# Turning h in two pieces of 768 and 640 columns, with an output product that starts on the first piece

## The chip, the cores and the metric

One Trainium2 chip, one core in use. The metric is the device time in microseconds (us) of one execution; the time before is the median of three runs.

## The reference

The input x is (32, 256, 512): 32 batches of 256 rows, 512 numbers each. Each batch goes through a cross attention with the context, and then each row of 512 through a feed-forward network whose operands are quantised to FP4 in blocks of 16. Cut to what matters here:

```
x = x + xattn(layernorm(x), ctx, ctx, Wt, Wp, Wg, Wz, gamma, beta)
# feed-forward, H = 512, I = 1408
gate = fp4_linear(layernorm(x), w_gate)        # (rows, 1408)
y    = fp4_linear(layernorm(x), w_up)          # (rows, 1408)
h    = silu(gate) * y
x    = x + fp4_linear(h, w_down)               # (rows, 512)
# fp4_linear(a, w) = fp4(a) @ fp4(w).T ; fp4: per block of 16 numbers,
# scale = max|.| / 6, each number rounded to {0, .5, 1, 1.5, 2, 3, 4, 6} * scale
```

## The kernel before

The rows are cut into 64 tiles of 128 rows (tile j, two tiles s = 0 and 1 to a batch i). All weights stay in SBUF. The engines run programs written out by hand, each with its own order; a loop over the batches 1 to 29 (`Fori(1, NB - 2)`) and two copies of its body for the last two batches make up nearly all of the time. Engines meet only at semaphores.

**TensorE (PE)**, per tile j: `scores(j + 2)` makes the attention products of a tile two ahead (L457), `hidden(j, s, c)` for c = 0 to 3 makes gate and up in four groups of 352 columns (L478, 24 matmuls a group), and `output(j - 1)` makes the down projection of the tile before (L489, 33 matmuls). Group c of `hidden` waits until VectorE has taken the group that stood in the same PSUM pair (`h_done`). Between the groups stand two tiny products for the attention's statistics: `group_means` (L465, waits for ScalarE's `rowst`) and `group_spread` (L470).

**What happens to h.** VectorE (DVE) multiplies silu and up into h (`gated`, L1126), takes block maxima and scales, and rounds h in place: `h_y` (L958), `h_snap_add` (L967), `h_snap_back` (L971). ScalarE (ACT) makes the grain of the rounding in between (L749). Then, in the next tile's turn of the loop, h is made ready for the product in two halves of 704 columns (`HPIECES`):

- `h_finish` (DVE, L975) writes hq, the quantised values in f32, one half after the other;
- `h_hi` (ACT, L734) rounds each half to f16, as soon as that half of hq is there;
- `h_lo` (DVE, L1113) subtracts the f16 part from hq, which leaves the low f16 part. It waits for `h_hi` of its half (L1112);
- `turn_h` (SyncE, SP, L383) waits for both halves and issues one transposing DMA of both parts, 22 blocks of 128 x 128, into `hT_parts`. `output` waits for it (`h_turned`).

The order on DVE in the loop body is: snap_add, snap_back, sum_pg, h_finish, h_lo, gated c = 0, normalise2 and the x quantisation of the next tile, gated c = 1, x_finish (its last step writes xq at L975), gated c = 2, x_lo, gated c = 3, then maxima, scales and `h_y` of this tile, residual, moments, and `emit` (L1135), which takes the output product. ACT's order is: copy_p, copy_u, `h_hi`, silu c = 0 (L781), u_moments (which end in `rowst`, L714), silu c = 1, the grain of x, `x_hi` (L728, waits for DVE's xq), silu c = 2, silu c = 3, affine, the grain of h. SP issues, per tile: a load, `turn_h`, `turn_x` (L376, 8 blocks), and the store.

After the last batch nothing is left to overlap: `h_snap_add` to `h_lo` of tile 63 on DVE and ACT, its `turn_h`, its 33 matmuls, its `emit` and its store follow one another.

Of the kernel before, what the change touches and what calls it, by code (L numbers as in the profile page):

```python
# [17 lines left out]
P = 128  # L18
F32 = mybir.dt.float32
F16 = mybir.dt.float16  # L20
BF16 = mybir.dt.bfloat16
# [18 lines left out]
def at_least(eng, sem, n):  # L40

    if isinstance(n, int) and n <= 0:
        return
    eng.wait_ge(sem, n)


def wait_apart(eng, always, sem, n):

    eng.wait_ge(always, 1)
    eng.wait_ge(sem, n)


def build(nc, x, ctx_in, Wt, Wp, Wg, Wz, gamma, beta, w_gate, w_up, w_down, out):
    NB, C, D = x.shape
    H = w_gate.shape[0]
# [5 lines left out]
    KH = H // P  # L63
# [10 lines left out]
    with ExitStack() as stack:  # L74
        def sb(name, shape, dt=F32):
            return stack.enter_context(nc.sbuf_tensor(name, shape, dt))
# [4 lines left out]
        def sem(name):  # L81
            return stack.enter_context(nc.semaphore(name))
# [5 lines left out]
        obank = work[:, 2]  # L88
# [20 lines left out]
        w2 = [w2_parts[:, part] for part in range(2)]  # L109
        up_staged = w2_parts[:].rearrange("p a k n -> p (a k n)").bitcast(F32)  # L110
        raw = sb("raw", [P, 3, HALF])
# [44 lines left out]
        hq = sb("hq", [P, H])  # L156
# [4 lines left out]
        h_row = sb("h_row", [P, 2])  # L161
        h_pow = sb("h_pow", [P, 2])
        o_unit = sb("o_unit", [P, 2])
        hT_parts = sb("hT_parts", [P, 2, KH, P], F16)
        hT = [hT_parts[:, part] for part in range(2)]
        o_sb = early[:, 2 * GW:].rearrange("p (a b) -> p a b", a=2)

        hq_parts = raw[:, 1, 0:H].bitcast(F16).rearrange("p (a k) -> p a k", a=2)
        xq_parts = raw[:, 1, H:H + D].bitcast(F16).rearrange("p (a k) -> p a k", a=2)
        HPIECES = ((0, H // 2), (H // 2, H))  # L170

        first_hm = hT_parts[:, 0].rearrange("p k n -> p (k n)").bitcast(BF16)


        consts_made = sem("consts_made")
# [6 lines left out]
        minus_made = sem("minus_made")  # L182
# [89 lines left out]
        h_t_done = sem("h_t_done")  # L272
        h_r_done = sem("h_r_done")
        hq_ready = sem("hq_ready")
        h_turned = sem("h_turned")
        h_hi_done = sem("h_hi_done")
        h_lo_done = sem("h_lo_done")
        o_done = sem("o_done")
# [65 lines left out]
        def _(sp):  # L344
# [33 lines left out]

            def turn_h(j):

                made = 2 * j + 2 if isinstance(j, int) else sp.to_reg(2 * j + 2)
                wait_apart(sp, minus_made, h_lo_done, made)
                sp.dma_start_transpose(hT_parts[:].rearrange("p a k n -> p (a k) n"),  # L383
                                       hq_parts.rearrange("p a k -> p (a k)")).then_inc(h_turned, 16)

            def store(j, s):
                sp.wait_ge(o_ready, j + 1)
# [53 lines left out]
        def _(pe):  # L441
# [41 lines left out]
            def output(j):  # L483

                at_least(pe, o_ready, j)
                pe.wait_ge(h_turned, 16 * j + 16)
                for k in range(KH):
                    for part, wpart in PARTS:
                        mm = pe.matmul(obank[:, :], hT[part][:, k, :], w2[wpart][:, k, :],  # L489
                                       start=(k == 0 and part == 0 and wpart == 0), stop=(k == KH - 1 and part == 1))  # L490
                mm.then_inc(o_done, 1)

# [195 lines left out]
            body(NB - 2)  # L688
            body(NB - 1)
            output(NT - 1)  # L690


        @block.scalar
        def _(act):
# [33 lines left out]
                nc.scalar.copy(xq_parts[:, 0, :], xq[:, :]).then_inc(x_hi_done, 1)  # L728

            def h_hi(j):  # L730
                at_least(act, h_turned, 16 * j)
                for r, (a, b) in enumerate(HPIECES):
                    act.wait_ge(hq_ready, 2 * j + r + 1)
                    nc.scalar.copy(hq_parts[:, 0, a:b], hq[:, a:b]).then_inc(h_hi_done, 1)  # L734

            def ctx_hi(b):
                act.wait_ge(c_loaded, 16 * b + 16)
# [217 lines left out]
        def _(dve):  # L955
# [154 lines left out]
            def h_lo(j):  # L1110
                for r, (a, b) in enumerate(HPIECES):
                    dve.wait_ge(h_hi_done, 2 * j + r + 1)  # L1112
                    nc.vector.tensor_tensor(hq_parts[:, 1, a:b], hq[:, a:b], hq_parts[:, 0, a:b],  # L1113
                                            ALU.subtract).then_inc(h_lo_done, 1)

            def x_lo(t):
# [432 lines left out]
```

## Time and profile before

| | |
|---|---|
| time, median of 3 runs | 1832.3 us (1831.49 to 1832.64) |
| the profiled execution: its own time | 1831.41 us |
| its span, first to last instruction | 1829.6 us |
| PE, DVE, ACT, POOL busy | 1745.3, 1653.1, 722.8, 800.8 us |
| mean TensorE clock granted | 0.994 |

The span is what the trace shows, the time holds in addition 1.8 us around it. A busy PE is not a PE at its peak: the records of matmuls that follow one another overlap. The waits say more than the busy shares: a view of the waits names, for each engine and line, what it waited for.

### The profile page before, as it was taken

Reading aid. Unit: us, or ns where it says so; the run is one execution under the profiler, and the core shown is the slowest. Engines: PE = TensorE matmul, PEld = TensorE weight load, DVE = VectorE, ACT = ScalarE, POOL = GpSimd, SP = SyncE. Lnnn points to the kernel's source line nnn. Section 1 sums busy time; section 2 is a strip of 40 time slices with the busy share of each in tenths; the row PEclk is TensorE's granted clock in tenths of the full one; section 3 lists DMA queues with packets and bytes.
Section 4 is the critical chain, followed back from the end, with each engine's and each line's share of the span. In section 5 each row is a group of like instructions: output and inputs, shape, how many; then the busy total and the mean of one; then the engine's idle time right before and its main releaser. Section 6 shows DMA issues by size and latency. Waiting matters only on the chain.

```text
span 1829.6 us, 30695 instructions
## 1 busy us (share of the span) xinstructions
PE 1745.3 (95%) x10124; PEld 1097.9 (60%) x10124; DVE 1653.1 (90%) x2629; ACT 722.8 (40%) x1246; POOL 800.8 (44%) x1069
## 2 busy tenths in 40 slices
PE   3799999999999999999999999999999999999996
PEld 2576656666666666566666666665666666666653
DVE  8999999999999999999999999999999999999984
ACT  3564344333434333344334333433433343443331
POOL 6884434344443434444443444443434444343300
PEclk9999999999999999999999999999999999999998
DMA  6112233222322332232233223223322332323122
GB/s 221 34 26 63 51 72 72 70 62 67 72 56 66 72 77 62 60 72 62 66 72 72 62 60 75 66 58 72 72 65 63 71 72 50 72 72 74 42 56 43
DMA packets 281879, 123.04 MB, mean 67 GB/s; under 512 B 252928, under 2 KB 254208, under 8 KB 281856
## 3 DMA queue, kind: packets, MB, share of 16 engines
q1 hardware_dynamic: 281856, 122.74, 28.3%
q8 instruction: 13, 0.21, 0.0%
q14 instruction: 10, 0.08, 0.0%
HBM read 43.03 MB, written 16.78 MB: 33 GB/s over the span
## 4 chain that ended last, share of the span: by engine, by line
PE 43%; DVE 34%; issue 14%; ACT 5%; DVEq 1%; POOL 1%; DMA 1%; ACTq 0%; SPq 0%; POOLq 0%
PE pairs L478 20%; PE work L489 13%; PE pairs L457 5%; DVE hq L975 3%; DVE q L997 3%; DVE h L1126 3%; DVE h L967 3%; ACT early L781 3%; DVE h L958 3%; PE ubank L457 3%; DVE h_amax L979 3%; ACT u_dev L711 1%; DVE x L1026 1%; DVE xn L971 1%; DVE ln_st L1030 1%
## 5 line engine op out<-in xcount | busy, mean ns | idle before, releaser
L478 PE MATMUL pairs<-w_gate_hi,xT_parts 128*128 128x352 f16 x2048 | 628.5, 313 | 12.1 <-DVE h L1126 12.0
L478 PE MATMUL pairs<-w_up_hi,xT_parts 128*128 128x352 f16 x2048 | 627.6, 312 | 0.0
L489 PE MATMUL work<-w_parts,hT_parts 128*128 128x512 f16 x2112 | 468.8, 380 | 12.9 <-DMA hT_parts<-raw 12.9
L489 PEld LDWEIGHTS work<-w_parts,hT_parts 128*128 128x128 f16 x2112 | 207.7, 100 | 250.0 <-issue 17.0
L478 PE MATMUL pairs<-w_up_lo,xT_parts 128*128 128x352 f16 x1024 | 320.0, 312 | 0.0
L478 PE MATMUL pairs<-w_gate_lo,xT_parts 128*128 128x352 f16 x1024 | 319.9, 312 | 0.0
L478 PEld LDWEIGHTS pairs<-w_gate_hi,xT_parts 128*128 128x128 f16 x2048 | 204.9, 100 | 137.7 <-DVE h L1126 23.7
L478 PEld LDWEIGHTS pairs<-w_up_hi,xT_parts 128*128 128x128 f16 x2048 | 200.4, 98 | 97.3
L1126 DVE SCALAR_TENSOR_TENSOR h<-pairs,w_unit,early 128x352 f32<-128x352 f32 x256 | 147.9, 578 | 87.3 <-ACT early L781 87.3
L781 ACT ACTIVATE early<-pairs,w_unit 128x352 f32<-128x352 f32 x256 | 141.1, 551 | 93.0 <-PE pairs L478 93.0
L734 ACT CAST raw<-hq 128x704 f16<-128x704 f32 x128 | 99.4, 778 | 176.1 <-DVE hq L975 174.8
L1392 POOL TENSOR_TENSOR xc<-x_in,c_in 128x512 f32<-128x512 f32 x64 | 163.6, 2576 | 0.0
L1397 POOL TENSOR_TENSOR c_lo<-c_in,c_hi 128x512 fp32r<-128x512 f32 x64 | 94.3, 1494 | 150.8 <-ACT c_hi L739 150.8
L1411 POOL TENSOR_TENSOR att<-rowst,grp 128x1 f32<-128x1 f32 x64 | 38.3, 598 | 268.2 <-DVE grp L1012 268.1
L749 ACT ACTIVATE wm<-h 128x1408 bf16<-128x1408 f32 x63 | 86.8, 1378 | 152.7 <-DVE h L958 152.7
L1433 POOL TENSOR_TENSOR ln_rs<-ln_mv,eps_col 128x1 f32<-128x1 f32 x64 | 13.6, 213 | 298.9 <-DVE ln_mv L1034 298.9
L971 DVE SCALAR_TENSOR_TENSOR h<-wm,h 128x1408 f32<-128x1408 bf16 x63 | 130.1, 2065 | 2.1
L720 ACT ACTIVATE v_sb<-u_sb,att 128x512 f32<-128x512 f32 x64 | 52.1, 814 | 201.5 <-POOL att L1429 201.5
L478 PEld LDWEIGHTS pairs<-w_up_lo,xT_parts 128*128 128x128 f16 x1024 | 100.1, 98 | 52.6
L478 PEld LDWEIGHTS pairs<-w_gate_lo,xT_parts 128*128 128x128 f16 x1024 | 100.1, 98 | 52.5
L975 DVE SCALAR_TENSOR_TENSOR hq<-h,h_unit 128x704 f32<-128x704 f32 x128 | 121.4, 988 | 0.1
L1113 DVE TENSOR_TENSOR raw<-hq,raw 128x704 f16<-128x704 f32 x128 | 108.4, 889 | 3.2
(154 smaller groups left out, 3044.2 us busy)
## 6 DMA issues: line engine op xcount, KB each, us to landing
x_in<-in_x SPq DMA_DIRECT2D x32, 512.0 KB, 3.4
c_in<-in_ctx SPq DMA_DIRECT2D x32, 512.0 KB, 3.5
out<-early SPq DMA_DIRECT2D x64, 256.0 KB, 2.1
raw<-in_L_ffn_w_down SPq DMA_DIRECT2D x2, 1408.0 KB, 8.8
raw<-in_L_ffn_w_gate SPq DMA_DIRECT2D x2, 1280.0 KB, 8.3
w_parts<-in_L_ffn_w_up SPq DMA_DIRECT2D x2, 1280.0 KB, 9.0
xT_parts<-raw SPq DMA_TRANSPOSE x64, 3.1
hT_parts<-raw SPq DMA_TRANSPOSE x64, 5.2
```

The lines of the kernel that those rows point to most:

```text
L457: mm = pe.matmul(dst, wT[wpart][:, k, s * P:(s + 1) * P], src[part][:, k, :], start=(k == 0 and wpart == 0 and part == 0), stop=(k == HT - ...
L478: mm = pe.matmul(pairs[:, pair, n, 0:GW], xT[s][part][:, k, :], w1[n][wpart][:, k, c * GW:(c + 1) * GW], start=(k == 0 and part == 0 and w ...
L489: mm = pe.matmul(obank[:, :], hT[part][:, k, :], w2[wpart][:, k, :], start=(k == 0 and part == 0 and wpart == 0), stop=(k == KH - 1 and pa ...
L734: nc.scalar.copy(hq_parts[:, 0, a:b], hq[:, a:b]).then_inc(h_hi_done, 1)
L749: nc.scalar.activation(m, y, ACT.Abs, scale=GRAIN).then_inc(done, 1)
L781: nc.scalar.activation(silu[:, c % 2, :], pairs[:, pair_of(j, s, c), 0, 0:GW], ACT.Silu, scale=w_unit[:, 0:1]).then_inc(silu_done, 1)
L971: nc.vector.scalar_tensor_tensor(out=y, in0=m, scalar=GRAIN, in1=y, op0=ALU.max, op1=ALU.subtract).then_inc(done, 1)
L975: nc.vector.scalar_tensor_tensor(out=blocks(q_out), in0=blocks(y), scalar=-factor, in1=over_block(scale), op0=ALU.mult, op1=ALU.mult).then ...
L1113: nc.vector.tensor_tensor(hq_parts[:, 1, a:b], hq[:, a:b], hq_parts[:, 0, a:b], ALU.subtract).then_inc(h_lo_done, 1)
L1126: nc.vector.scalar_tensor_tensor(out=h[:, c * GW:(c + 1) * GW], in0=pairs[:, pair_of(j, s, c), 1, 0:GW], scalar=w_unit[:, 1:2], in1=silu[: ...
L1392: nc.gpsimd.tensor_tensor(xc[:, s, :], x_in[:, s, :], c_in[:, s, :], ALU.add).then_inc(xc_ready, 1)
L1397: nc.gpsimd.tensor_tensor(c_parts[1][:, s, :], c_in[:, s, :], c_parts[0][:, s, :].bitcast(F32), ALU.subtract).then_inc(c_ready, 1)
```

## The change

`HPIECES` becomes (0, 768) and (768, 1408), that is 6 and 5 blocks of 128 columns instead of 704 and 704. The hi and lo parts of a piece lie side by side, so that a piece is one contiguous stretch (12 blocks with both parts, then 10). `turn_h` issues one transposing DMA for each piece as soon as `h_lo` of the piece is done, each with its own semaphore. `output` waits for the first before its first matmul and for the second before its 19th. `h_hi` waits before each piece until the earlier transpose of that piece is over. The number of DVE, ACT and PE instructions that compute stays the same; only their sizes change.

```diff
--- before.py
+++ after.py
@@ -161,15 +161,23 @@
         h_row = sb("h_row", [P, 2])
         h_pow = sb("h_pow", [P, 2])
         o_unit = sb("o_unit", [P, 2])
-        hT_parts = sb("hT_parts", [P, 2, KH, P], F16)
-        hT = [hT_parts[:, part] for part in range(2)]
+        hT_parts = sb("hT_parts", [P, 2 * KH, P], F16)
         o_sb = early[:, 2 * GW:].rearrange("p (a b) -> p a b", a=2)
 
-        hq_parts = raw[:, 1, 0:H].bitcast(F16).rearrange("p (a k) -> p a k", a=2)
+        hq_parts = raw[:, 1, 0:H].bitcast(F16)
         xq_parts = raw[:, 1, H:H + D].bitcast(F16).rearrange("p (a k) -> p a k", a=2)
-        HPIECES = ((0, H // 2), (H // 2, H))
-
-        first_hm = hT_parts[:, 0].rearrange("p k n -> p (k n)").bitcast(BF16)
+        HPIECES = ((0, 6 * P), (6 * P, H))
+
+        def hq_part(r, part):
+            a, b = HPIECES[r]
+            return hq_parts[:, 2 * a + part * (b - a):2 * a + (part + 1) * (b - a)]
+
+        def hT(part, k):
+            a, b = HPIECES[0] if k < 6 else HPIECES[1]
+            return hT_parts[:, (2 * a + part * (b - a)) // P + k - a // P, :]
+
+
+        first_hm = hT_parts[:, 0:KH].rearrange("p k n -> p (k n)").bitcast(BF16)
 
 
         consts_made = sem("consts_made")
@@ -272,7 +280,7 @@
         h_t_done = sem("h_t_done")
         h_r_done = sem("h_r_done")
         hq_ready = sem("hq_ready")
-        h_turned = sem("h_turned")
+        h_turned = [sem(f"h_turned{r}") for r in range(2)]
         h_hi_done = sem("h_hi_done")
         h_lo_done = sem("h_lo_done")
         o_done = sem("o_done")
@@ -378,10 +386,10 @@
 
             def turn_h(j):
 
-                made = 2 * j + 2 if isinstance(j, int) else sp.to_reg(2 * j + 2)
-                wait_apart(sp, minus_made, h_lo_done, made)
-                sp.dma_start_transpose(hT_parts[:].rearrange("p a k n -> p (a k) n"),
-                                       hq_parts.rearrange("p a k -> p (a k)")).then_inc(h_turned, 16)
+                for r, (a, b) in enumerate(HPIECES):
+                    made = 2 * j + r + 1 if isinstance(j, int) else sp.to_reg(2 * j + r + 1)
+                    wait_apart(sp, minus_made, h_lo_done, made)
+                    sp.dma_start_transpose(hT_parts[:, 2 * a // P:2 * b // P, :], hq_parts[:, 2 * a:2 * b]).then_inc(h_turned[r], 16)
 
             def store(j, s):
                 sp.wait_ge(o_ready, j + 1)
@@ -483,10 +491,11 @@
             def output(j):
 
                 at_least(pe, o_ready, j)
-                pe.wait_ge(h_turned, 16 * j + 16)
                 for k in range(KH):
+                    if k in (0, 6):
+                        pe.wait_ge(h_turned[k // 6], 16 * j + 16)
                     for part, wpart in PARTS:
-                        mm = pe.matmul(obank[:, :], hT[part][:, k, :], w2[wpart][:, k, :],
+                        mm = pe.matmul(obank[:, :], hT(part, k), w2[wpart][:, k, :],
                                        start=(k == 0 and part == 0 and wpart == 0), stop=(k == KH - 1 and part == 1))
                 mm.then_inc(o_done, 1)
 
@@ -728,10 +737,10 @@
                 nc.scalar.copy(xq_parts[:, 0, :], xq[:, :]).then_inc(x_hi_done, 1)
 
             def h_hi(j):
-                at_least(act, h_turned, 16 * j)
                 for r, (a, b) in enumerate(HPIECES):
+                    at_least(act, h_turned[r], 16 * j)
                     act.wait_ge(hq_ready, 2 * j + r + 1)
-                    nc.scalar.copy(hq_parts[:, 0, a:b], hq[:, a:b]).then_inc(h_hi_done, 1)
+                    nc.scalar.copy(hq_part(r, 0), hq[:, a:b]).then_inc(h_hi_done, 1)
 
             def ctx_hi(b):
                 act.wait_ge(c_loaded, 16 * b + 16)
@@ -1110,7 +1119,7 @@
             def h_lo(j):
                 for r, (a, b) in enumerate(HPIECES):
                     dve.wait_ge(h_hi_done, 2 * j + r + 1)
-                    nc.vector.tensor_tensor(hq_parts[:, 1, a:b], hq[:, a:b], hq_parts[:, 0, a:b],
+                    nc.vector.tensor_tensor(hq_part(r, 1), hq[:, a:b], hq_part(r, 0),
                                             ALU.subtract).then_inc(h_lo_done, 1)
 
             def x_lo(t):
```

SP's program in the first half of the loop body, before. A transpose of 22 blocks stands between the load of x and the transpose of x:

```order
L349 ISA [waits xc_ready,q_norm]
L349 DMA x_in<-in_x 128x2x512
L381 ISA
L383 DMA_TRANSPOSE hT_parts<-raw 128x22x128 [waits h_lo_done,minus_made]
L374 REGISTER_ALU
L376 DMA_TRANSPOSE xT_parts<-raw 128x8x128 [waits x_lo_done,minus_made]
L388 ISA [waits o_ready]
L388 DMA out<-early 128x512
```

The same place now:

```order
L357 ISA [waits xc_ready,q_norm]
L357 DMA x_in<-in_x 128x2x512
L390 ISA
L392 DMA_TRANSPOSE hT_parts<-raw 128x12x128 [waits h_lo_done,minus_made]
L390 REGISTER_ALU
L392 DMA_TRANSPOSE hT_parts<-raw 128x10x128 [waits h_lo_done,minus_made]
L382 REGISTER_ALU
L384 DMA_TRANSPOSE xT_parts<-raw 128x8x128 [waits x_lo_done,minus_made]
L396 ISA [waits o_ready]
L396 DMA out<-early 128x512
```

One row of 22 blocks has become two, of 12 and of 10, each behind its own value of `h_lo_done`. Nothing else on SP has changed places.

ACT's program, the two casts of `h_hi` between the copy of u (L703, now L712) and silu c = 0 (L781, now L790), before:

```order
L703 ACTIVATE u_sb,u_sum<-ubank 128x512 [waits v_ready,u_done]
L734 CAST raw<-hq 128x704 [waits hq_ready,h_turned]
L734 CAST raw<-hq 128x704 [waits hq_ready]
L781 ACTIVATE early<-pairs,w_unit 128x352 [waits h_done,gu_done]
L709 ACTIVATE rowst<-u_sum 128x1 [waits u_copied,sq_steps,grp_done]
```

And now:

```order
L712 ACTIVATE u_sb,u_sum<-ubank 128x512 [waits v_ready,u_done]
L743 CAST raw<-hq 128x768 [waits hq_ready,h_turned0]
L743 CAST raw<-hq 128x640 [waits hq_ready,h_turned1]
L790 ACTIVATE early<-pairs,w_unit 128x352 [waits h_done,gu_done]
L718 ACTIVATE rowst<-u_sum 128x1 [waits u_copied,sq_steps,grp_done]
```

The first cast has grown from 704 to 768 columns, the second has shrunk to 640 and has one more semaphore to wait for. On DVE the four instructions L975, L975, L1113, L1113 stand where they stood and change their sizes in the same way.

PE's program at the output product in the loop, before:

```order
L470 MATMUL ubank<-att,gmean 128x1 [waits grp_copied,sq_steps]
L489 MATMUL work<-w_parts,hT_parts 128x512 [waits h_turned,o_ready]
L489 MATMUL work<-w_parts,hT_parts 128x512 x32
L686 REGISTER_ALU
L686 COMPARE_AND_BRANCH
L457 MATMUL pairs<-q_hi,wpT_hi 128x512 [waits q_ready,h_done]
```

And now:

```order
L478 MATMUL ubank<-att,gmean 128x1 [waits grp_copied,sq_steps]
L498 MATMUL work<-w_parts,hT_parts 128x512 [waits h_turned0,o_ready]
L498 MATMUL work<-w_parts,hT_parts 128x512 x17
L498 MATMUL work<-w_parts,hT_parts 128x512 [waits h_turned1]
L498 MATMUL work<-w_parts,hT_parts 128x512 x14
L695 REGISTER_ALU
L695 COMPARE_AND_BRANCH
L465 MATMUL pairs<-q_hi,wpT_hi 128x512 [waits q_ready,h_done]
```

The 33 matmuls are the same, in the same order; a second wait stands before the 19th.

## Rows read from the trace of the kernel before

**Rows 1.** The page: span and busy time of each engine

```profile
span 1829.6 us, 30695 instructions
...
PE 1745.3 (95%) x10124; PEld 1097.9 (60%) x10124; DVE 1653.1 (90%) x2629; ACT 722.8 (40%) x1246; POOL 800.8 (44%) x1069
```

**Rows 2.** 300 us of the loop: PE, PEld, DVE, ACT, POOL busy (calls)

```profile
200.00:500.00 300.00, 295.93 (x1719) 184.06 (x1718) 276.67 (x451) 119.38 (x208) 129.59 (x178) 1.00 0.29 67
```

**Rows 3.** Waits of PE and DVE, 200 to 1780 us

```profile
PE ubank L465 <- ACT rowst L714: 12.4, 29, 0.4
PE pairs L478 <- DVE h L1126: 9.9, 29, 1.4
...
DVE h L1126 <- ACT early L781: 76.7, 64, 2.3
```

**Rows 4.** DVE in order of time, 880 to 960 us

```profile
889.60 1.69 DVE L975 SCALAR_TENSOR_TENSOR hq<-h,h_unit 128x704 f32<-128x704 f32 x2
891.33 1.69 DVE L1113 TENSOR_TENSOR raw<-hq,raw 128x704 f16<-128x704 f32 x2
892.94 0.57 DVE L1126 SCALAR_TENSOR_TENSOR h<-pairs,w_unit,early 128x352 f32<-128x352 f32 x1
...
926.18 0.69 DVE L975 SCALAR_TENSOR_TENSOR xq<-xn,x_scale 128x512 f32<-128x512 f32 x1
928.09 0.58 DVE L1126 SCALAR_TENSOR_TENSOR h<-pairs,w_unit,early 128x352 f32<-128x352 f32 x1 [1.22 <-ACT early L781]
...
945.96 0.58 DVE L1126 SCALAR_TENSOR_TENSOR h<-pairs,w_unit,early 128x352 f32<-128x352 f32 x1
```

**Rows 5.** ACT in order of time, same stretch

```profile
890.51 1.58 ACT L734 CAST raw<-hq 128x704 f16<-128x704 f32 x2 [1.93 <-DVE hq L975]
...
926.98 0.62 ACT L728 CAST raw<-xq 128x512 f16<-128x512 f32 x1 [2.29 <-DVE xq L975]
927.50 0.55 ACT L781 ACTIVATE early<-pairs,w_unit 128x352 f32<-128x352 f32 x1
```

**Rows 6.** Durations by line: ns min/median/max

```profile
L975 DVE SCALAR_TENSOR_TENSOR hq<-h,h_unit x128: 877/884/1355, 137.2 to 1808.2; 128x704 f32<-128x704 f32 x128
L975 DVE SCALAR_TENSOR_TENSOR xq<-xn,x_scale x64: 691/691/1643, 85.1 to 1771.1; 128x512 f32<-128x512 f32 x64
...
L734 ACT CAST raw<-hq x128: 777/778/782, 152.8 to 1809.2; 128x704 f16<-128x704 f32 x128
...
L728 ACT CAST raw<-xq x64: 617/618/622, 88.2 to 1771.8; 128x512 f16<-128x512 f32 x64
```

**Rows 7.** The two transposing DMAs: issue in ns, us to landing

```profile
L383 SPq DMA_TRANSPOSE hT_parts<-raw x64: 3237/3342/3398, 155.4 to 1811.0; - x64
...
DMA to landing us min/median/max: 5.1/5.2/6.9
...
L376 SPq DMA_TRANSPOSE xT_parts<-raw x64: 1232/1232/1391, 89.8 to 1774.1; - x64
...
DMA to landing us min/median/max: 3.0/3.1/3.2
```

**Rows 8.** Chain that ended last, from 1780 us: start, us, what

```profile
1786.72 0.78 DVE raw L1113
...
1809.23 1.70 DVE raw L1113 x2
...
1810.99 5.17 DMA hT_parts<-raw
...
1816.30 10.01 PE work L489 x33
```

**Rows 9.** Weight loads of the last tile's output

```profile
1816.27 0.14 PEld L489 LDWEIGHTS work<-w_parts,hT_parts 128*128 128x128 f16 x2 [13.34 <-issue]
...
1821.80 4.00 PEld L489 LDWEIGHTS work<-w_parts,hT_parts 128*128 128x128 f16 x19 [0.28 <-issue]
```

**Rows 10.** 4 us near the end, columns as in Rows 2, then clock

```profile
1807.00:1811.00 4.00, 0.00 (x0) 0.00 (x0) 3.79 (x5) 1.52 (x2) 0.00 (x0) 0.65 0.00 0
```

## The prediction

> **What bounds the kernel now.** The page comes first [rows 1]: PE is busy for 95% of the span, DVE for 90%. In a stretch from the middle of the loop PE is busy for 295.93 of 300 us and DVE for 276.67 [rows 2]. This looks like a kernel bound by PE, and it is nearly one. The view of the waits says otherwise [rows 3]. Between 200 and 1780 us PE waits 29 times for `rowst` before `group_means` (12.4 us, 0.43 each) and 29 times for DVE's `gated` before a group of `hidden` (9.9 us): once each in a batch of two tiles, in 29 batches. DVE, in the same stretch, waits 64 times for ACT's silu (76.7 us, 1.2 each) and never for PE.
>
> What is this wait of DVE for silu? The timelines of DVE and ACT show one instance [rows 4, 5]. DVE writes xq at 926.18; ACT, whose order puts `x_hi` ahead of silu c = 2, has waited 2.29 us for xq, casts it at 926.98 and runs silu at 927.50; DVE goes on with `gated` at 928.09. So the wait starts from DVE's own work and comes back to DVE over ACT, and PE has no part in it. DVE's program with its trips to ACT is a closed ring that sets the period: `gated` c = 0 starts at 892.94 in one batch and at 945.96 in the next, 53.02 us [rows 4]. PE keeps up with some 0.4 us to spare in a tile. What makes DVE's ring longer is paid in every tile; what comes earlier on SP, the DMA queues or PE inside the loop is worth nothing.
>
> A second regime is the end. There the chain is: `h_lo` at 1809.23 for 1.70 us, the transpose from 1810.99 for 5.17, and 33 matmuls from 1816.30 for 10.01 [rows 8]. Each step waits for all of the one before.
>
> **The change in the loop: earlier transposes.** The first DMA can be issued one `h_lo` piece earlier. In the loop nothing waits for it: of PE's waits between 200 and 1780 us none is for `hT_parts` [rows 3]. Worth 0, hidden by PE's own groups c = 0 to 3. The second DMA costs SP one more issue; SP issues 22 blocks in 3.342 us and 8 in 1.232 [rows 7], 0.151 a block with almost nothing fixed, so two pieces take what one took. `turn_x` stands behind it on SP, and needs `x_lo`, for which DVE has three `gated` and the whole quantisation of x to do first. Cost 0. PE's new wait before matmul 19 has long been met and costs 0; ACT's new wait too.
>
> **The change in the loop: the sizes on the ring.** This is the part that I think decides. `h_finish` writes hq in two pieces, ACT casts the first as soon as it stands, and DVE's `h_lo` begins with this first piece. So between the start of `h_finish` and the start of `h_lo` there are two paths: DVE's two pieces of hq (the sum of both, unchanged), and the first piece of hq followed by the first cast. With halves the two are even. From [rows 4, 5]: hq starts at 889.60 and both pieces end at 891.29. The first piece takes 0.884 us [rows 6], to 890.48; ACT starts at 890.51, takes 0.778, and ends at 891.29 as well; `h_lo` starts at 891.33. A first piece of 768 columns makes the second path longer and leaves the first as it is.
>
> How much longer: DVE's same instruction takes 884 ns for 704 columns and 691 for 512 [rows 6], 1.005 ns a column, 64 ns for 64 columns. ACT's cast takes 778 ns for 704 and 618 for 512 [rows 6], 0.833 a column, 53 ns. Together 0.118 us: `h_lo` would start at 891.45. What follows doesn't win it back: the two pieces of `h_lo` together have as many columns as before; the second cast is through by 892.2, before the second `h_lo` could start (892.3); and `gated` c = 0 waits for `h_lo` alone.
>
> How often: `h_lo` runs in the loop body for 62 tiles. The waits of PE for DVE and ACT, two in a batch, mark 29 batches, 58 tiles, as bound by this ring [rows 3]. I add the last two tiles, where the chain that ended last runs over `h_lo` [rows 8], and leave the first two, where DVE hasn't yet become the later one. 60 x 0.118 = **7.1 us lost**. Bounds: 0 if something absorbs it; above, in tiles in which GpSimd slows the first piece of hq (1355 ns for 704 columns at most [rows 6], 1.92 a column), the 64 columns would cost 0.123 on DVE and not 0.064. In one tile of each batch that is 30 x 0.06 = 1.8 more. I take 7.1, since the extra columns are at the piece's end, when GpSimd is mostly done.
>
> **The change at the end.** The first `h_lo` starts 0.12 later, at 1809.35, and takes 0.95 for 768 columns (0.890 plus 64 more at the rate above), to 1810.30; the transpose is issued 0.06 later as now, at 1810.36, 0.63 earlier than 1810.99 [rows 8]. Landing takes 5.2 us for 22 blocks and 3.1 for 8 [rows 7]: 0.15 a block on 1.9, so 3.7 for 12 blocks, 1.5 less. PE starts at 1814.2 instead of 1816.3. The second piece is issued when SP is through with the first (1812.2) and lands 3.4 later, at 1815.6; PE wants it at about 1820.8. So the end is **2.1 us shorter**. Bounds: a landing of 3.1 (as 8 blocks) gives 2.7, one of 5.2 gives 0.6.
>
> The matmuls there start on a slow clock. PE's clock goes from full to the lower of its two levels (1.2 and 2.4 GHz) before the transpose lands: the mean granted is 0.65 in 1807 to 1811 [rows 10], which puts the fall near 1808.2. In the product 13 weight loads from 1816.27 to 1821.80 are 0.425 us apart, and the rest 0.216 [rows 9]. With the pause before the product's first weight load shortened from 13.3 us [rows 9] to 11.2 the fall, at 1808.2, still comes first, so I keep the 13 slow matmuls. The Trainium skill, TensorE: Matmul & The Clock Gate, "Part 1: The HAM clock gate", says that this number changes from run to run, and names 6, 11 and 14 slow matmuls for one kernel; this trace has one such product, with 13, and can't show the spread. By that page's 6 the sum would be 1.5 us lower, by its 14 0.2 higher.
>
> **Sum.** 7.1 - 2.1 = 5.0 us. Against the profiled execution's own time, 1831.41 (span 1829.6 and 1.8 around it), that is 1836.4; the median of the runs is 0.9 above that execution, so the forecast for the median is 1832.3 + 5.0 = **1837.3 us**, 0.27% slower. A measurement of this kernel can tell about 0.2%, 3.7 us, from no change.
>
> **The rivals.**
> - *Slack on DVE absorbs the delay* (not slower). This needs a wait of DVE behind `h_lo` that doesn't hang on `h_lo`, of at least 0.12 us in a tile. For it: the busy shares, PE 98.6% and DVE 92% [rows 2]. Against it: all of DVE's waits of any size are the trip over ACT, which starts from DVE. Then only the end counts: 1832.3 - 2.1 = 1830.2, with bounds 1829.6 and 1831.7. Chance 0.10, a third of it below the 0.2%.
> - *Half of the tiles absorb it*: the tile of a batch in which GpSimd works beside DVE gives the time back, because GpSimd goes on while DVE waits, and slows DVE less after. 30 x 0.118 - 2.1 = +1.4, 1833.7. Chance 0.10.
> - *The clock comes back earlier at the end*: 6 slow matmuls in place of 13 save 7 x 0.21 = 1.5. The sum is +3.5, 1835.8, on the edge. The only recovery in the rows took 5.5 us. Chance 0.08.
> - *The change does not do at the end what it says*: the two transposes share the DMA engines, and the first lands when a single one would have (5.2 after issue). Gain 0.6; +6.5, 1838.8. Speaking for it: only that no row shows two transposes in flight. Chance 0.07.
> - *A second wait on the ring*: the second cast, now with two semaphores and started after a longer first one, ends after 892.3 and holds the second `h_lo`, or GpSimd slows the longer piece. 0.03 to 0.1 us a tile, 2 to 6 us more: about 1841. Margin now 0.15 us a tile. Chance 0.09.
> - *The forecast* as summed: 0.56, with a range of its own of 1835.7 to 1839.
>
> **How the numbers follow.** The forecast is slower by over 0.2% in nearly nine of ten of its cases, since its terms may be off by 1.3 us (0.50 of 0.56); the slow clock's case in half (0.04), the two dearer cases fully (0.16): slower 0.70. Faster: 0.04. Same: the rest, 0.26. A range from 1833.3 to 1840.5 leaves out the first rival, half of the dearest and little else.
>
> **What the profile of the changed kernel would show.** Right: the period from `gated` c = 0 to the same of the next batch at 53.26 instead of 53.02; DVE's `h_lo` of the first piece starting 0.16 after hq's end, not 0.04, with ACT's cast as releaser, some 10 us of idle time in all; PE's waits for `rowst` and `gated` longer by as much; hq pieces of 948 and 820 ns, casts of 831 and 725; at the end the first transpose landing 3.7 after its issue and PE starting 5 us after the first `h_lo` does. Wrong: a period of 53.02 (absorbed); a later start of the second `h_lo` than the first's end (dearer); a landing of over 4.5 us at the end.

## The result and the profile after

The changed kernel takes 1837.72 us in the median of 7 runs (1837.55 to 1838.74), the one before 1831.49 in 7 runs (1830.93 to 1832.99). The ratio is 1.0033 with a 95% interval from 1.0022 to 1.0045: slower by 6.2 us, forecast 5.0. The profiled execution has a span of 1836.4 us and a time of 1838.19; before they were 1829.6 and 1831.41, so that the two traces, 6.8 us apart, hold the whole difference.

The page of the changed kernel, its head (answers to [rows 1]), and its waits of PE and DVE between 200 and 1780 us (to [rows 3]; engine, line, what it waited for, total us, times, longest):

```profile
span 1836.4 us, 30886 instructions
...
PE 1744.1 (95%) x10124; PEld 1097.4 (60%) x10124; DVE 1655.7 (90%) x2629; ACT 717.0 (39%) x1246; POOL 788.1 (43%) x1069
```

```profile
DVE h L1135 <- ACT early L790: 75.0, 62, 2.3
...
PE pairs L486 <- DVE h L1135: 20.9, 29, 1.5
...
PE ubank L473 <- ACT rowst L723: 11.1, 29, 0.4
...
DVE raw L1122 <- ACT raw L743: 10.0, 60, 0.2
```

The busy times have hardly moved. What has moved are waits. A row is there that wasn't: DVE's `h_lo` (now L1122) waits for ACT's cast 60 times, 0.17 us each. And PE waits for DVE's `gated` 20.9 us in place of 9.9, and for `rowst` 11.1 in place of 12.4: 9.7 us more for the two together.

DVE of the changed kernel in order of time, the same place in a batch as in [rows 4], with the two starts of `gated` c = 0 that bound a batch, and ACT's casts (to [rows 5]):

```profile
893.54 1.69 DVE L984 SCALAR_TENSOR_TENSOR hq<-h,h_unit 128x768 f32<-128x768 f32 x2
895.39 1.69 DVE L1122 TENSOR_TENSOR raw<-hq,raw 128x768 f16<-128x768 f32 x2 [0.16 <-ACT raw L743]
897.00 0.58 DVE L1135 SCALAR_TENSOR_TENSOR h<-pairs,w_unit,early 128x352 f32<-128x352 f32 x1
...
950.38 0.58 DVE L1135 SCALAR_TENSOR_TENSOR h<-pairs,w_unit,early 128x352 f32<-128x352 f32 x1
```

```profile
894.52 1.46 ACT L743 CAST raw<-hq 128x768 f16<-128x768 f32 x2 [2.18 <-DVE hq L984]
```

From the start of hq to the start of `h_lo` it is 895.39 - 893.54 = 1.85 us; it was 891.33 - 889.60 = 1.73 [rows 4]. That is the 0.12 of the forecast. But the batch, from 897.00 to 950.38, takes 53.38 us, and the forecast had 53.26.

The end, as the chain that ended last (start, us, what; to [rows 8]), and the weight loads of the last output (to [rows 9]):

```profile
1816.84 0.97 DVE hq L984
...
1817.88 0.84 ACT raw L743
...
1818.75 0.97 DVE raw L1122
...
1819.78 3.72 DMA hT_parts<-raw
...
1823.64 9.43 PE work L498 x33
```

```profile
1823.61 0.14 PEld L498 LDWEIGHTS work<-w_parts,hT_parts 128*128 128x128 f16 x2 [11.28 <-issue]
...
1827.86 4.70 PEld L498 LDWEIGHTS work<-w_parts,hT_parts 128*128 128x128 f16 x22 [0.28 <-issue]
```

The transpose of 12 blocks lands 3.72 us after its issue where 22 took 5.17. From the start of the last hq to the first matmul it is 1823.64 - 1816.84 = 6.80 us; it was 8.86 (1816.30 less 1807.44, the start of the last hq before). The product itself takes 9.43 us where it took 10.01: 10 weight loads 0.425 apart, where there were 13.

**Where the 6.8 us are.** In the two traces, from the first `h_lo` of the loop (tile 1) to that of tile 62 it was 1610.6 us before (176.13 to 1786.72), and is 1620.1 now (176.01 to 1796.12): 9.5 lost in 61 tiles. The way from there to the last hq is 20.72 us in both. The end gives 2.06 back by the earlier start and 0.58 by three fewer slow matmuls. 9.5 - 2.6, and 0.1 less before the loop, is 6.8.

### The profile page after: what moved, and what is told of

Read it like the earlier page. It is cut to its first block, busy times and chain, and to the rows that moved or that the text cites. A ratio compares the mean times of both kernels' runs of the same rounds, so it can differ in the third digit from the quotient of the medians.

```text
span 1836.4 us, 30886 instructions
## 1 busy us (share of the span) xinstructions
PE 1744.1 (95%) x10124; PEld 1097.4 (60%) x10124; DVE 1655.7 (90%) x2629; ACT 717.0 (39%) x1246; POOL 788.1 (43%) x1069
## 4 chain that ended last, share of the span: by engine, by line
DVE 60%; issue 22%; PE 8%; ACT 6%; DVEq 2%; DMA 1%; POOL 0%; ACTq 0%; SPq 0%; POOLq 0%
DVE h L976 5%; DVE h L967 5%; DVE h_amax L988 5%; DVE h L1135 4%; PE pairs L486 4%; DVE hq L984 4%; ACT raw L743 3%; DVE xn L980 2%; DVE ln_st L1039 2%; DVE x L1035 2%; DVE x_amax L988 2%; DVE x_scale L991 2%; DVE xq L984 2%; DVE raw L1127 2%; DVE xn L976 2%
## 5 line engine op out<-in xcount | busy, mean ns | idle before, releaser
L498 PE MATMUL work<-w_parts,hT_parts 128*128 128x512 f16 x2112 | 468.2, 380 | 10.8 <-DMA hT_parts<-raw 10.8
L790 ACT ACTIVATE early<-pairs,w_unit 128x352 f32<-128x352 f32 x256 | 141.1, 552 | 84.9 <-PE pairs L486 84.9
L743 ACT CAST raw<-hq 128x768 f16<-128x768 f32 (+1 forms) x128 | 93.4, 777 | 183.9 <-DVE hq L984 183.9
L1406 POOL TENSOR_TENSOR c_lo<-c_in,c_hi 128x512 fp32r<-128x512 f32 x64 | 81.7, 1297 | 149.3 <-ACT c_hi L748 149.3
L984 DVE SCALAR_TENSOR_TENSOR hq<-h,h_unit 128x768 f32<-128x768 f32 (+1 forms) x128 | 121.4, 988 | 0.1
L1122 DVE TENSOR_TENSOR raw<-hq,raw 128x768 f16<-128x768 f32 (+1 forms) x128 | 108.4, 888 | 10.8 <-ACT raw L743 10.8
```

What stands on the lines that cost most here:

```text
L498: mm = pe.matmul(obank[:, :], hT(part, k), w2[wpart][:, k, :], start=(k == 0 and part == 0 and wpart == 0), stop=(k == KH - 1 and part == 1))
L743: nc.scalar.copy(hq_part(r, 0), hq[:, a:b]).then_inc(h_hi_done, 1)
L790: nc.scalar.activation(silu[:, c % 2, :], pairs[:, pair_of(j, s, c), 0, 0:GW], ACT.Silu, scale=w_unit[:, 0:1]).then_inc(silu_done, 1)
L984: nc.vector.scalar_tensor_tensor(out=blocks(q_out), in0=blocks(y), scalar=-factor, in1=over_block(scale), op0=ALU.mult, op1=ALU.mult).then ...
L1122: nc.vector.tensor_tensor(hq_part(r, 1), hq[:, a:b], hq_part(r, 0), ALU.subtract).then_inc(h_lo_done, 1)
```

## The experiments

Each run of the kernel before on the same chips had medians of 1830.6 to 1831.4 us; ratios are to those. Twelve runs follow, of eleven kernels: one was run twice.

### Sizes without a second DMA: sizes_alone

```diff
-        HPIECES = ((0, H // 2), (H // 2, H))
+        HPIECES = ((0, 6 * P), (6 * P, H))       # in the kernel before, nothing else
```

> The kernel before with pieces of 768 and 640 columns for hq, the cast and h_lo, and still one transposing DMA after both and one wait in the output. My theory (the first piece and its cast lie on a ring of DVE and ACT that sets the period): h_lo starts 0.16 us after the end of hq in every tile, the period is 53.38 us as in the changed kernel, the loop loses its 9.5 us, and the end gains nothing (0.1 lost): about 1841 us, 3 more than the changed kernel. The rival (the second DMA and the added waits cost the time in the loop, the sizes nothing): 1831.5, as before.

Measured: 1842.24 us against 1830.94, ratio 1.0063 (1.0049 to 1.0076). The steps from one `h_lo` to the next are the changed kernel's to 0.01 us, 25.13 and 28.23 in turn, where before they were 25.01 and 28.01. The whole loss in the loop is there without a second DMA and without a second wait on PE, ACT or SP. The time is 1.2 above the 1841 expected.

### Two DMAs without the sizes: hi_then_lo

```diff
-                made = ...(2 * j + 2)
-                wait_apart(sp, minus_made, h_lo_done, made)
-                sp.dma_start_transpose(hT_parts[...], hq_parts[...]).then_inc(h_turned, 16)
+                for part, done in enumerate((h_hi_done, h_lo_done)):
+                    made = ...(2 * j + 2)
+                    wait_apart(sp, minus_made, done, made)
+                    sp.dma_start_transpose(hT_parts[:, part], hq_parts[:, part, :]).then_inc(h_turned[part], 16)
...
+                pe.wait_ge(h_turned[0], 16 * j + 16)     # 22 matmuls with the high part
...
+                pe.wait_ge(h_turned[1], 16 * j + 16)     # then 11 with the low part
```

> Two transposing DMAs and two waits in the output, but halves of 704 columns as before: the first DMA takes all 11 blocks of the high part as soon as ACT has cast both halves, the second the low part; the output does its 22 matmuls with the high part first. My theory: the loop is as before (period 53.02); at the end the first DMA is issued 1.0 us earlier and lands in 3.55 and not 5.17, so that PE starts 2.6 us earlier, and the slow clock's matmuls stay 11 to 13: 1828.9 us. The rival (DMAs and waits cost the loop 9.5 us): about 1838.5.

Measured: 1828.18 us against 1830.94, ratio 0.9985 (0.9976 to 0.9994). The loop has the steps of before, 25.01 and 28.0. The end, as the chain of this kernel, starts its product 6.29 us after the last hq (before 8.86):

```profile
1807.03 0.90 DVE hq L979
...
1808.03 1.51 ACT raw L738 x2
...
1809.61 3.58 DMA hT_parts<-raw
...
1813.32 6.24 PE work L489 x22
1819.56 2.39 PE work L493 x11
```

ACT's cast of both halves releases the DMA, `h_lo` is no longer on the way. Seven matmuls run at the lower clock here, where I had expected 11 to 13. This is the first version that beats both kernels: it keeps what the change gains and has nothing of what it costs.

### The ring opened: silu_first and silu_first_pieces

```diff
-                        if c == 1 and (more or s == 0):
+                        if c == 2 and (more or s == 0):
                             x_hi(j + 1)                  # behind silu c = 2 on ACT, in the loop body
```

> The kernel before with one move on ACT: silu c = 2 runs before x_hi and not behind it. DVE's wait of 1.22 us a tile, which I take for part of a ring without PE, should shrink to about 0.1. My theory (DVE's ring sets the period, PE has 0.8 us to spare in a batch of 53.02): the loop becomes bound by PE at about 52.2 us a batch, some 24 us less in all, 1808 us (1804 to 1814). The rival (PE is the bound of the loop in truth and DVE's waits are idle time without a price): 1831.5.

> The same move on ACT made in the changed kernel (768 and 640 columns, two DMAs). My theory: with DVE's ring no longer the bound, the 0.12 us that the sizes add to a tile is absorbed and only the gain at the end is left, so that this is 2.6 us faster than silu_first: about 1805 us. The rivals (the change costs PE or the DMA queues time in the loop whatever bounds it): 6 us slower than silu_first.

Measured: silu_first 1799.17 us, ratio 0.9824 (0.9811 to 0.9837); silu_first_pieces 1799.58, 0.9829 (0.9817 to 0.9842). The waits of silu_first between 200 and 1740 us:

```profile
DVE h L1126 <- ACT early L781: 22.8, 61, 2.4
...
DVE raw L1118 <- ACT raw L728: 15.3, 58, 0.3
...
PE pairs L478 <- DVE h L1126: 1.3, 1, 1.3
```

And those of silu_first_pieces, of the same stretch:

```profile
DVE h L1135 <- ACT early L790: 19.3, 61, 2.4
...
DVE raw L1127 <- ACT raw L737: 15.4, 58, 0.3
...
DVE raw L1122 <- ACT raw L743: 9.9, 60, 0.2
...
PE pairs L486 <- DVE h L1135: 1.5, 1, 1.5
```

PE waits once in the whole stretch where it waited twice a batch. The period is 51.93 us in both kernels, 24.51 and 27.42 in turn. So DVE's ring set the period, and a trip of 1.2 us over ACT was worth 32 us of the whole; I had expected 24, since I had put PE's own need at 52.2 a batch and not at 51.9, and 1799.17 lies below the range of 1804 to 1814 that I had given.

The second kernel is the sharper test. It has the same 0.16 us before `h_lo` in each of 60 tiles as the changed kernel, 9.9 us in all, and its period is not longer by 0.01. The same pieces cost the loop 9.5 us where DVE is the bound and nothing where PE is.

One part of the expectation failed: silu_first_pieces should have been 2.6 us faster than its partner, and was 0.4 slower, well within the noise of the two intervals. Its last output does start 2.0 us earlier (1782.95 against 1784.92), but takes 10.01 us and not 8.70: 13 slow matmuls against 7. The next two groups follow this up.

### Does PE's slow clock hide the gain at the end? silu_warm and silu_warm_pieces

```diff
             body(NB - 1)
+            pe.wait_ge(h_done, GROUPS * NT)
+            pe.wait_ge(o_ready, NT - 1)
+            for n in range(42):
+                pe.matmul(pairs[:, 0, 0, :], minus_ident[:, :], w2[0][:, n % KH, :], start=True, stop=True)
             output(NT - 1)
```

> silu_first (halves of 704, one DMA) with 42 matmuls of 512 columns on PE that nothing reads, between the output of tile 62 and that of tile 63, so that PE does not rest in the wait at the end. Silu_first had 7 slow matmuls in the last output (8.7 us for 33), the changed kernel 10, before and silu_first_pieces 13. My theory: with no slow matmul the output takes 7.1 us; 1.6 us less than silu_first's profile, 1797.6 us. It serves as the base of the next run.

> The same 42 matmuls in silu_first_pieces (the change). Silu_first_pieces started its last output 2.0 us earlier than silu_first, but took 10.0 us for it and not 8.7, and was no faster in the median. My theory: only the number of slow matmuls hid the gain; with none in either this is 2.0 us faster than silu_warm: 1795.6 us. If something else eats the gain at the end: equal to silu_warm.

Measured: silu_warm 1801.24 us (1797.2 to 1801.33), silu_warm_pieces 1796.42 (1795.11 to 1797.6). The first missed: it is slower than silu_first. Its weight loads at the end:

```profile
1773.01 8.76 PEld L693 LDWEIGHTS pairs<-w_parts,minus_ident 128*128 128x128 f16 x42 [1.40 <-issue]
1784.95 0.34 PEld L489 LDWEIGHTS work<-w_parts,hT_parts 128*128 128x128 f16 x3 [3.18 <-issue]
1785.49 0.15 PEld L489 LDWEIGHTS work<-w_parts,hT_parts 128*128 128x128 f16 x1 [0.20 <-issue]
...
1788.82 4.63 PEld L489 LDWEIGHTS work<-w_parts,hT_parts 128*128 128x128 f16 x22 [0.19 <-issue]
```

PE rests 3.18 us between the last filling matmul and the output; the first three loads are close, then come loads 0.425 apart. The clock fell about when the output began: the mean granted is 0.91 in 1782 to 1786 and 0.66 in 1786 to 1790. In silu_warm_pieces, with the same 42 matmuls, the rest is 1.10 us, and no load is slow. The pair therefore differs by more than the start, and by itself says nothing of the 2.0 us.

### The same with equal rests: silu_warm52, silu_warm_pieces_again, silu_warm_hilo

The filling has 52 matmuls in silu_warm52 and 38 in silu_warm_hilo, which joins silu_first and hi_then_lo.

> silu_warm with 52 filling matmuls and not 42. Silu_warm missed its purpose: PE rested 3.2 us between the last filling matmul and the last output, the clock fell at its start, and 9 matmuls were slow (8.98 us for the output, 1801.2 us in the median), while with the change's earlier transpose (silu_warm_pieces, a rest of 1.1 us) none was slow (7.30, 1796.4). With 52 the rest is about 1 us. My theory: no slow matmul, 7.2 us for the output, and a time 2.0 us above silu_warm_pieces, that is 1798.4 on the same chip. If the gain at the end were no gain: equal to silu_warm_pieces.

> The same kernel as silu_warm_pieces, on the same chip as silu_warm52, as its partner: 1796.4 us.

> The version to which the experiments point: silu c = 2 ahead of x_hi, halves of 704 columns, the high part turned first and the low part second (hi_then_lo), 38 filling matmuls. In hi_then_lo the last output started 6.2 us after the last hq, in the pieces 6.8, in the halves with one DMA 8.9. My theory: 0.6 us faster than silu_warm_pieces at the end, and 0.1 in each of the last two tiles: 1795.6 us; the rival, that the two are equal since the loop is bound by PE in both: 1796.4.

Measured: silu_warm52 1797.23 us (1797.11 to 1799.6), silu_warm_pieces_again 1795.48 (1795.27 to 1796.43), silu_warm_hilo 1795.09 (1794.74 to 1797.48). Weight loads at the end of silu_warm52, then of silu_warm_pieces_again:

```profile
1772.76 10.92 PEld L693 LDWEIGHTS pairs<-w_parts,minus_ident 128*128 128x128 f16 x52 [1.40 <-issue]
1784.70 6.82 PEld L489 LDWEIGHTS work<-w_parts,hT_parts 128*128 128x128 f16 x33 [1.02 <-issue]
```

```profile
1772.98 8.76 PEld L702 LDWEIGHTS pairs<-w_parts,minus_ident 128*128 128x128 f16 x42 [1.40 <-issue]
1782.86 6.82 PEld L498 LDWEIGHTS work<-w_parts,hT_parts 128*128 128x128 f16 x33 [1.12 <-issue]
```

The products take 7.30 us in both, and with the clock out of the way the earlier transpose is worth 1.75 us of 2.0 expected; in the traces the product starts 7.07 us after `h_lo` in the one and 4.88 in the other, 2.2 less. Silu_warm_hilo is the fastest kernel of the study, ratio 0.9805 (0.9792 to 0.9819) to the kernel before; its lead of 0.4 on silu_warm_pieces_again is not clear of the noise.

### The wait before h_lo filled: norm_between

```diff
                     h_finish(j - 1)
+                    if quant_x:
+                        normalise2(j + 1)
                     h_lo(j - 1)
                     for c in range(GROUPS):
                         gated(j, s, c)
                         if c == 0 and quant_x:
-                            normalise2(j + 1)
                             x_first(j + 1)              # in the changed kernel
```

> The changed kernel with one move on DVE: normalise2 of the next tile (0.53 us, ready long before) stands between h_finish and h_lo instead of behind gated c = 0, so that DVE has work while ACT casts the first piece. My theory: the idle 0.16 us before h_lo goes, also the 0.08 by which instructions that wait for nothing overlap; a tile is 0.24 shorter than in the changed kernel and 0.12 shorter than before, and the gain at the end stays: 1837.7 - 60 x 0.24 = 1823 us, 8 faster than before; what GpSimd does to DVE may move it by 2. If the cost of the change in the loop were not this wait: 1837.7.

Measured: 1821.89 us, ratio 0.995 (0.9937 to 0.9964). DVE of this kernel around `h_finish`:

```profile
887.39 1.69 DVE L984 SCALAR_TENSOR_TENSOR hq<-h,h_unit 128x768 f32<-128x768 f32 x2
889.00 0.54 DVE L1049 TENSOR_SCALAR xn<-x,ln_mv,ln_rs 128x512 f32 x1
889.45 1.69 DVE L1122 TENSOR_TENSOR raw<-hq,raw 128x768 f16<-128x768 f32 x2
891.05 0.58 DVE L1135 SCALAR_TENSOR_TENSOR h<-pairs,w_unit,early 128x352 f32<-128x352 f32 x1
```

No idle time stands before `h_lo`; each instruction starts some 0.09 us before the one ahead has ended, as do those that wait for nothing. The steps are 24.74 and 27.95, 52.69 a batch where the changed kernel has 53.36. The change's whole loss in the loop is gone, and more, with all of the change in place.

Not all of this gain is the wait. From the start of hq to the start of the block maxima of x (`x_amax`, L988) it is 4.16 us here (887.39 to 891.55) and 4.53 in the changed kernel (893.54 to 898.07), 0.37 less where I had expected 0.24. The further 0.12 comes from normalise2 itself: in the changed kernel the maxima, which read its result, start 0.57 us after it, and here the next instruction starts 0.45 after it. The kernel before should gain this 0.12 too; it was not run with the move. Behind this stretch, in the tile in which GpSimd works on the context, 0.10 is lost again (from `x_amax` to `gated` c = 1 it is 4.61 us, in the changed kernel 4.51). The 0.25 that is left is still more than the 0.12 that the change had added to a tile, so DVE stood idle for a cast that it could have worked beside.

### Why 9.5 and not 7.1: sizes_736

```diff
-        HPIECES = ((0, H // 2), (H // 2, H))
+        HPIECES = ((0, 736), (736, H))           # in the kernel before
```

> The kernel before with pieces of 736 and 672 columns (32 more and less, where the change has 64) and one transposing DMA. sizes_alone showed the step from one h_lo to the next 0.12 longer in one tile of a batch and 0.23 in the other. If all of it is the path over the first piece and its cast, both are proportional to the columns: 0.06 and 0.115 longer, 5 us in all. If the part above 0.12 is a step, because a different DVE instruction falls under GpSimd's, 0.06 and either 0.06 or 0.17: 3.6 or 6.9 us in all.

Measured: 1832.59 us against 1830.64, ratio 1.0013 (1.0004 to 1.0023). The steps are 25.07 and 28.01: 0.06 longer in one tile, as expected, and not longer at all in the other. Neither of my two accounts had this. The stretch in question lies behind `gated` c = 0 in the tile in which ACT casts the context (L739) and GpSimd then subtracts it (L1397, `ctx_lo`, two instructions, 1.27 us each in the changed kernel). DVE's groups of instructions between 200 and 1740 us (name, shape, count, busy us, mean ns), of the kernel before:

```profile
L958 DVE SCALAR_TENSOR_TENSOR xn<-xn,x_rinv 128x512 f32<-128x512 f32 x58 | 58.1, 1002 | 2.0
L997 DVE TENSOR_SCALAR q<-x_in,ln_mv,ln_rs 128x512 f32<-128x512 f32 x58 | 56.4, 1013 | 0.0
...
L982 DVE TENSOR_SCALAR x_scale<-x_amax 128x32 f32<-128x32 f32 x58 | 10.5, 181 | 2.0
```

Of the changed kernel:

```profile
L967 DVE SCALAR_TENSOR_TENSOR xn<-xn,x_rinv 128x512 f32<-128x512 f32 x58 | 58.4, 1007 | 2.0
...
L991 DVE TENSOR_SCALAR x_scale<-x_amax 128x32 f32<-128x32 f32 x58 | 39.7, 685 | 2.0
...
L1006 DVE TENSOR_SCALAR q<-x_in,ln_mv,ln_rs 128x512 f32<-128x512 f32 x58 | 29.7, 550 | 0.0
```

The three together were 1002 + 1013 + 181 = 2196 ns in the mean of a tile, and are 1007 + 685 + 550 = 2242: 2.7 us more in 58 tiles. That is the missing part of the 9.5. With 736 columns they are 978, 1013 and 181, that is 1.4 us less in 58 tiles, 0.05 a batch: the absorbed 0.06. DVE and GpSimd of the changed kernel in the tile with `ctx_lo`:

```profile
898.70 2.49 POOL L1406 TENSOR_TENSOR c_lo<-c_in,c_hi 128x512 fp32r<-128x512 f32 x2 [5.13 <-ACT c_hi L748]
...
898.79 1.22 DVE L991 TENSOR_SCALAR x_scale<-x_amax 128x32 f32<-128x32 f32 x1
...
900.43 1.31 DVE L967 SCALAR_TENSOR_TENSOR xn<-xn,x_rinv 128x512 f32<-128x512 f32 x1
```

The scale (L991, 32 columns) is 0.18 us in the other tile, and here 1.22. It starts 0.09 us after GpSimd's subtraction and ends with the first of its two instructions. In the kernel before the two start 0.10 us the other way round, the scale is through, and L958 and `q` are held in its place:

```profile
894.72 0.18 DVE L982 TENSOR_SCALAR x_scale<-x_amax 128x32 f32<-128x32 f32 x1
...
894.82 2.95 POOL L1397 TENSOR_TENSOR c_lo<-c_in,c_hi 128x512 fp32r<-128x512 f32 x2 [5.19 <-ACT c_hi L739]
...
895.32 1.32 DVE L958 SCALAR_TENSOR_TENSOR xn<-xn,x_rinv 128x512 f32<-128x512 f32 x1
```

With 736 columns they start together, 894.99 and 895.00, and the scale still takes 0.18. So the traces differ in which of DVE's instructions meets GpSimd. The shift between the two engines is 0.19 us, and most of it is the change's: from the start of hq to `gated` c = 0 DVE takes 3.46 us where it took 3.34, while ACT, which releases GpSimd, is through with its two casts 2.44 us after the start of hq where it took 2.49.

### GpSimd's subtraction taken away: small_ctx_pieces

```diff
+                w = D if isinstance(b, int) and b < 3 else 8            # in the changed kernel
-                    nc.gpsimd.tensor_tensor(c_parts[1][:, s, :], c_in[:, s, :], ...
+                    nc.gpsimd.tensor_tensor(c_parts[1][:, s, 0:w], c_in[:, s, 0:w], ...
```

> The changed kernel, but GpSimd's subtraction ctx_lo (L1406) works on 8 of 512 columns from batch 3 on; the other columns of the context's low part are left as they were, so this part of the computation is left out. My account: in the changed kernel DVE stands still during GpSimd's two subtractions of 1.27 us. The traces have, as means over 58 tiles between 200 and 1740 us, x_scale 685 ns, xn at L967 1007 ns and q at L1006 550 ns (2242 together), and in the kernel before 181, 1002 and 1013 (2196 together), which is 2.7 us in 58 tiles more. If GpSimd's subtraction is what holds them, x_scale now takes 0.18 us, xn 0.69 and q 2 x 0.5 in both tiles of a batch, 3.9 us from gated c = 0 to gated c = 1 where it was 5.58. Rival: what holds them is something else (a memory bank shared with PE or ACT, a transfer); then x_scale still takes 1.22 in every second tile, and the batch stays near 53.4. Time by my account: DVE's ring would need 53.38 - 1.66 = 51.72 a batch, PE needed 51.93 in silu_first; with the tiles taken apart, 25.13 (ring) and 27.42 (PE) make 52.55. So 0.8 to 1.45 us a batch less, 29 batches: 1796 to 1814 us. By the rival 1838.

Measured: 1796.22 us against 1831.37, ratio 0.9807 (0.979 to 0.9823). The same place in the trace of this kernel:

```profile
880.32 0.37 POOL L1407 TENSOR_TENSOR c_lo<-c_in,c_hi 128x8 fp32r<-128x8 f32 x2 [5.14 <-ACT c_hi L748]
880.40 0.18 DVE L991 TENSOR_SCALAR x_scale<-x_amax 128x32 f32<-128x32 f32 x1
...
881.01 0.69 DVE L967 SCALAR_TENSOR_TENSOR xn<-xn,x_rinv 128x512 f32<-128x512 f32 x1
```

The scale takes 0.18, L967 0.69, and from `gated` c = 0 (878.62) to c = 1 it is 3.91 us where the changed kernel has 5.58 (897.00 to 902.58) and the kernel before 5.49 (892.94 to 898.43). It was GpSimd's subtraction that held DVE, 1.67 us a batch in the changed kernel and, if its same instructions too need 3.91 when nothing holds them, 1.58 in the kernel before. The difference is the 0.09 a batch that the sum of the prediction lacks. The batch takes 51.9 us, no longer DVE's ring but PE's own need as in silu_first; so the whole can't show what the 1.67 would be worth beyond that.

The Trainium skill speaks of it (GPSIMD Engine Reference, "1. Specifications"): VectorE and GpSimd share interfaces to SBUF, and get in each other's way when the VectorE instruction is in a 2-port mode or reads two SBUF inputs. The traces agree that they hold each other up: GpSimd's second subtraction takes 1.27 us (median) in the changed kernel and 1.72 in the kernel before, where DVE's `q` (from 896.56) runs beside it. The scale reads one tensor, and no row tells its mode.

## Why the prediction was right

- *DVE's ring over ACT sets the period, PE does not*: right. Opening it gave 31.8 us (silu_first), and the change's idle time was free there (silu_first_pieces).
- *DMAs, issue on SP and the added waits cost 0 in the loop*: right; hi_then_lo has them all and keeps the period, sizes_alone has none of them and loses as much.
- *The first piece and its cast delay `h_lo` by 0.118 us a tile*: right to 0.01 (1.73 to 1.85 us). The bound: `h_lo` of the second piece never waited.
- *60 tiles, 7.1 us*: the step that was mis-sized. Between the `h_lo` of tile 1 and that of tile 62, 57 of the 61 steps became longer (28 batches and one of the last two tiles); the first two of the loop absorb the delay, as said, and two near the end too, where the batch has no context to prepare. That makes 6.7. The delay of the very last tile lies in the end, where the prediction counts it a second time (`h_lo` 0.12 later). The loop lost 9.5, because in 28 of these tiles the delay also moved DVE deeper under GpSimd's subtraction, 0.10 more each: 2.8 by the steps, 2.7 by the mean durations, and the interval in question fell to 3.91 us once the subtraction was taken away (small_ctx_pieces). The prediction had GpSimd in its upper bound (1.8 more), but at another place, the first piece of hq. That piece's 1355 ns became 1419, 64 more, so there the extra columns cost what I took.
- *2.1 us shorter end*: 2.06 by the start, to which 0.58 came from 10 slow matmuls in place of 13. The forecast kept 13. The number isn't fixed by the rest of PE before the product: after rests of 13.3 to 13.5 us the traces show 13, 13, 13 and 7, after 11.3 us 13, 11, 10 and 8, and after 10.8 us 7. So these 0.58 us can't be put down to the change.
- *Of the rivals*, slack on DVE and the tile that absorbs the delay were both wrong for 768 columns. The second was right for 736 (sizes_736: 0 in one tile of two), by GpSimd as its mechanism said. The rival with fewer slow matmuls came in by 3 of its 7. Of the two dearer ones, the first transpose landed 3.72 us after its issue and not 5.2, and no second wait appeared; a loss of the size of that second rival (2 to 6 us more) did come, at a place that it doesn't name.
- The two errors of the sum, 2.4 us too little lost and 0.5 too little gained, leave 6.8 in the traces and 6.2 in the medians against 5.0. That the time forecast, 1837.3, is only 0.4 from the one measured is partly luck: the kernel before was put at 1832.3 and came out at 1831.49 beside the changed one.

## What to carry to other kernels

An engine that is busy for 98.6% of a stretch need not be its bound: look for the wait that begins and ends on the same other engine (DVE to ACT to DVE here), and price every edit on that ring by what it adds to it. When one engine hands pieces to another and takes them back, the size of the first piece is on the ring even if the sum of the sizes is not; put something else between the hand-over and the return, as norm_between does. A shift of 0.2 us can also change which instruction meets another engine's; compare mean durations by form, not only waits. And an edit that gains at the end of a program only should touch nothing that each turn of the loop pays for: the same gain was to be had by turning the high part first.

## What the runs showed of the hardware that was not expected

- A DVE instruction of 0.18 us (32 columns, L991) took 1.22 when it started 0.09 us after a GpSimd subtraction of two SBUF tensors, ended when that did, and took 0.18 again once the subtraction had 8 columns. The price of meeting GpSimd isn't proportional to the DVE instruction; here it is near what is left of GpSimd's: 1.04 us more with 1.18 left, and for L967, which meets the second subtraction, 0.62 more with 0.77 left. When the scale started with GpSimd or 0.1 us ahead of it, it took 0.18.
- The last product had 7 to 13 matmuls at the lower clock, 1.2 of 2.4 GHz, after rests of 10.8 to 13.5 us, 0.21 us each more; gains of 2 us at the end are of the size of this. With a rest of 3.2 us the clock fell once, with rests of 1.0 to 1.5 us it did not.
- In the profiled executions of norm_between and silu_warm_pieces the first `h_lo` of the loop comes at 178.7 and 178.4 us, in all others at 175.8 to 176.3. These 2.5 us arise before the loop. In both the mean granted clock was 0.57 between 50 and 62 us, where PE prepares the weights, and in the others 0.72 to 1.00. No run shows that the clock is the whole cause; the time before the loop is part of the scatter of the medians.
